# First chunk of a fused attention and gated feed-forward block: scales found from three groups of maxima, weight halves shared between engines, another order around the first gate and up products

## The reference

```python
xn = _layernorm(x)
# attention, 16 heads of 16 channels
q, k, v = split(xn @ Wq.T), split(xn @ Wk.T), split(xn @ Wv.T)
q, k = elu(q) + 1.0, elu(k) + 1.0
kv_state = einsum('bhnd,bhne->bhde', k, v)      # sums over all 1024 tokens
k_state = k.sum(axis=2)
attn = einsum('bhnd,bhde->bhne', q, kv_state) / maximum(einsum('bhnd,bhd->bhn', q, k_state), 1e-6)
local = conv over 3 neighbouring tokens of xn, per channel (conv_w, conv_b)
a = (attn + local) @ Wp.T + bp
# feed-forward, 768 hidden channels, weights int32 in -127..127, scale 1/127
h = silu(xn @ wg.T) * (xn @ wu.T)
out = x + a + h @ wd.T
```

## Time and profile before

| what | us |
|---|---|
| median of 3 runs (507.33 to 507.74) | 507.38 |
| time of the profiled execution | 506.9 |
| its span, first to last instruction | 505.3 |
| TensorE busy (share of the span) | 491.4 (97%) |
| VectorE / ScalarE / GpSimd busy | 430.5 / 334.3 / 144.7 |
| granted TensorE clock, mean | 0.999 |
| mean of one silu, L536 (ScalarE) | 0.687 |
| mean of one hidden, L896 (VectorE) | 0.744 |
| mean of one high half, L544 (ScalarE) | 0.622 |
| mean of one low half, L902 (VectorE) | 0.691 |

### The profile page before, as it was taken

How to read it: one execution, slowest core, us unless ns; L and a number is a source line. 1 busy time by engine, 2 the same in 40 slices (tenths; PEclk the granted TensorE clock), 3 DMA queues, 4 the chain that set the end, 5 groups by cost and what they waited for, 6 DMA issues and landing times.

```text
span 505.3 us, 11017 instructions
## 1 busy us (share of the span) xinstructions
PE 491.4 (97%) x3968; PEld 306.1 (61%) x3968; DVE 430.5 (85%) x833; ACT 334.3 (66%) x522; POOL 144.7 (29%) x152
## 2 busy tenths in 40 slices
PE   7888999999999999999999999999999999999997
PEld 6545364755747566474756657475565756657576
DVE  4889898889888898988889888889888889897786
ACT  2676866667485775757667485667758576674770
POOL 3563415140321405033140502314041141401050
PEclk9999999999999999999999999999999999999999
DMA  8573434333524423252352325233342442233012
GB/s 307 183 91 77 86 82 87 68 111 51 151 43 111 99 45 125 41 166 42 83 125 42 125 42 164 43 82 100 54 138 42 126 82 42 87 50 74 3 42 84
DMA packets 68653, 45.36 MB, mean 90 GB/s; under 512 B 33424, under 2 KB 68112, under 8 KB 68624
## 3 DMA queue, kind: packets, MB, share of 16 engines
q1 hardware_dynamic: 59360, 35.79, 25.2%
q0 software_dynamic: 8448, 8.39, 11.0%
q10 hardware_dynamic: 816, 0.79, 0.5%
HBM read 20.32 MB, written 8.39 MB: 57 GB/s over the span
## 4 chain that ended last, share of the span: by engine, by line
PE 88%; DVE 5%; ACT 3%; DMA 2%; issue 1%; ACTq 0%; DVEq 0%
PE ps L1202 16%; PE ps L1039 16%; PE ps L1211 15%; PE ps L1221 15%; PE ps L1145 15%; PE ps L1101 5%; PE ps L1110 3%; PE ps L1164 2%; DMA wv_raw<-in_L_attn_Wv_dram 2%; DVE maxima L665 1%; DVE hl L902 1%; DVE hid L896 1%; ACT hh L544 1%; DVE cb L764 0%; PE ps L1085 0%
## 5 line engine op out<-in xcount | busy, mean ns | idle before, releaser
L536 ACT ACTIVATE act_g<-ps,scales 128x512 f32<-128x512 f32 x96 | 65.9, 687 | 42.0 <-PE ps L1211 39.7
L896 DVE SCALAR_TENSOR_TENSOR hid<-act_g,scales,ps 128x512 f32<-128x512 f32 x96 | 71.4, 744 | 21.2 <-ACT act_g L536 20.7
L902 DVE TENSOR_TENSOR hl<-hid,hh 128x512 f16<-128x512 f32 x96 | 66.3, 691 | 1.8 <-ACT hh L544 0.4
L361 POOL TENSOR_TENSOR xT<-xh,xl 128x1024 f32<-128x1024 f16 x15 | 32.3, 2153 | 109.4 <-issue 109.4
L544 ACT ACTIVATE hh<-hid 128x512 f16<-128x512 f32 x96 | 59.7, 622 | 5.3 <-DVE hid L896 5.3
L1202 PE MATMUL ps<-xh,g_wh 128*128 128x512 f16 x192 | 57.6, 382 | 2.1 <-ACT u_wh L455 1.4
L1211 PE MATMUL ps<-xl,g_wh 128*128 128x512 f16 x192 | 57.1, 379 | 0.0
L1202 PE MATMUL ps<-xh,u_wh 128*128 128x512 f16 x192 | 57.1, 379 | 0.0
L1211 PE MATMUL ps<-xl,u_wh 128*128 128x512 f16 x192 | 57.1, 379 | 0.0
L1221 PE MATMUL ps<-d_wh,hh 128*128 128x256 f16 x384 | 52.4, 273 | 2.2 <-DVE hid L896 2.2
L499 ACT ACTIVATE k_neg<-ps,scales 128x512 f32<-128x512 f32 x30 | 20.6, 687 | 49.4 <-PE ps L1145 49.4
(11 more groups left out here) (149 smaller groups left out, 965.5 us busy)
## 6 DMA issues: line engine op xcount, KB each, us to landing
xb<-bp_sb SPq DMA_DIRECT2D x16, 512.0 KB, 3.4
xb<-in_L_attn_x_dram POOLq DMA_DIRECT2D x16, 512.0 KB, 5.9
x_in<-in_L_attn_x_dram SPq DMA_DIRECT2D x15, 512.0 KB, 4.1
out_dram<-out_sb SPq DMA_DIRECT2D x14, 512.0 KB, 2.9
out_dram<-out_sb SPq DMA_DIRECT2D x4, 256.0 KB, 2.1
wg_int<-in_L_ffn_w_gate_dram SPq DMA_DIRECT2D x1, 768.0 KB, 7.1
wu_int<-in_L_ffn_w_up_dram SPq DMA_DIRECT2D x1, 768.0 KB, 8.6
wd_int<-in_L_ffn_w_down_dram SPq DMA_DIRECT2D x1, 768.0 KB, 11.1
```

The source lines that it names most:

```text
L536: nc.scalar.activation(act_g[:, j % 2, :], ps[:, gate_bank(j), :], ACT.Silu, scale=silu_in).then_inc(silu_ready, 1)
L896: nc.vector.scalar_tensor_tensor(out=hid[:, j % 2, :], in0=act_g[:, j % 2, :], scalar=h_mul, in1=ps[:, gate_bank(j) + 1, :], op0=ALU.mult, ...
L902: nc.vector.tensor_tensor(hl[:, j, :], hid[:, j % 2, :], hh[:, j, :], ALU.subtract).then_inc(hl_ready, 1)
```

## The change

The down weights' group and the last one become one group, so there are three. VectorE makes the second half of u_wh, ScalarE the first; ScalarE makes v_wh and k_wh, between silu(0) and the first half of the next chunk's x; ScalarE makes four of the six parts of d_wh and GpSimd two. GpSimd adds the first pair of keys once the gate and up weights are ready and the second pair after the next chunk's rstd. On TensorE the turn of the second group has another PSUM bank and waits no more for the first group's scales; its spread stands one place earlier; the two `accumulate` stand behind pairs 2 and 3; the register of the down weights is loaded ahead of `gate_up(5)` instead of ahead of `down(0)`. The scales of the attention need no `powers` of their own. In the second chunk `relu_q` stands ahead of the outer taps. In every chunk GpSimd's sum xT is four instructions. At the end the last output is made and stored in two halves, the second stored from ScalarE's queue.

```diff
-        GROUPS = [["k", "v", "q"], ["g", "u"], ["d"], ["cw", "cb", "p"]]
+        GROUPS = [["k", "v", "q"], ["g", "u"], ["d", "cw", "cb", "p"]]
...
-        MAX_BANK = [7, 7, 7, STATE]
+        MAX_BANK = [7, STATE, 7]
...
             run(sp, step)
+            for c, p in ((0, 0), (0, 1), (1, 0)):
+                store_pair(NB - 1, c, p)
+            sp.wait_ge(out_ready, NB * CB * 2)
+            sp.dma_start(out_v[NB * CB - 1][:, 2, :], out_sb[:, 1, 2, :]).then_inc(out_stored[1], 16)
             for c in range(CB):
-                for p in range(2):
-                    store_pair(NB - 1, c, p)
-            for c in range(CB):
-                sp.wait_ge(out_stored[c], 16 * NB + 16)
+                sp.wait_ge(out_stored[c], 16 * NB + 16 + 16 * c)
...
+                    if c == 1:
+                        first_keys(1)
...
-                nc.gpsimd.tensor_tensor(xT[:, c, :, 1:1 + CHUNK].rearrange("p k (i t) -> p i k t", i=TILES),
-                                        xh[:, c, :, :, :], xl[:, c, :, :, :], ALU.add).then_inc(xT_ready, 1)
+                for i in range(TILES):
+                    ins = nc.gpsimd.tensor_tensor(xT[:, c, :, 1 + i * P:1 + (i + 1) * P], xh[:, c, i, :, :],
+                                                  xl[:, c, i, :, :], ALU.add)
+                ins.then_inc(xT_ready, 1)
...
+            def first_keys(p):
+
                 pool.wait_ge(k_parts, p + 1)
                 nc.gpsimd.tensor_tensor(k_sb[:, 2 * p:2 * p + 2, :], k_exp[:, p, :, :], k_relu[:, p, :, :],
                                         ALU.add).then_inc(k_ready, 1)
+
+            pool.wait_ge(gate_up_seen, 1)
+            pool.sem_inc(norms_due, 1)
+            pool.wait_ge(gate_up_hi, 3)
+            first_keys(0)
...
+                        pool.wait_ge(scaled[2], 1)
+                        pool.sem_inc(norms_due, 1)
+                        nc.gpsimd.tensor_scalar(d_w[0][:, D_BY_ACT:J, :],
+                                                ffn_raw["d"][:, D_BY_ACT * D:J * D].rearrange("p (k n) -> p k n", n=D),
+                                                col(scale_up, "d"), None, ALU.mult).then_inc(d_hi, 1)
...
                 if past:
                     query_parts()
                 else:
-                    high(u_w[0][:, :, :], ffn_raw["u"][:, :].rearrange("p (k n) -> p k n", k=KT), "u", gate_up_hi)
+                    high(u_w[0][:, 0, :], ffn_raw["u"][:, 0:HID], "u", gate_up_hi)
                 nc.scalar.preload_act_table(ACT.Silu)
...
+                    if j == 0 and not past:
+                        high(kv_w[0][:, :, D:2 * D], w_raw["v"][:, :, :], "v", v_hi)
+                        high(kv_w[0][:, :, 0:D], w_raw["k"][:, :, :], "k", k_hi)
                     if j == D_SPLIT and not past:
-                        high(d_w[0][:, :, :], ffn_raw["d"][:, :].rearrange("p (k n) -> p k n", k=J), "d", d_hi)
+                        high(d_w[0][:, 0:D_BY_ACT, :],
+                             ffn_raw["d"][:, 0:D_BY_ACT * D].rearrange("p (k n) -> p k n", n=D), "d", d_hi)
...
             run(act, step)
+            act.wait_ge(out_ready, NB * CB * 2 + 1)
+            act.dma_start(out_v[NB * CB - 1][:, 3, :], out_sb[:, 1, 3, :]).then_inc(out_stored[1], 16)
...
+                nc.vector.tensor_tensor(cb[:, :], cb_raw[:, :], y_up.broadcast_to([P, KT]), ALU.mult).then_inc(taps_made, 1)
+                nc.vector.scalar_tensor_tensor(out=cw[:, :, :], in0=cw_raw[:, :, :], scalar=1.0 / X_UP,
+                                               in1=y_up.unsqueeze(2).broadcast_to([P, KT, 3]), op0=ALU.mult,
+                                               op1=ALU.mult).then_inc(taps_made, 1)
...
+            def last_output(banks):
+
+                dve.wait_ge(wp_done, NB * CB * 2)
+                dve.wait_ge(res_ready, NB * CB * 2)
+                dve.wait_ge(out_stored[1], (NB - 1) * 16)
+                for i in range(2):
+                    nc.vector.scalar_tensor_tensor(out=out_sb[:, 1, 2 + i, :], in0=ps[:, banks[1], i * D:(i + 1) * D],
+                                                   scalar=y_down, in1=res[:, 1, 2 + i, :],
+                                                   op0=ALU.mult, op1=ALU.add).then_inc(out_ready, 1)
...
-                    gate_up_high("g", g_w)
+                    gate_up_high("g", g_w[0][:, :, :], ffn_blocks("g", KT))
+                    gate_up_high("u", u_w[0][:, 1, :], ffn_raw["u"][:, HID:2 * HID])
                     stats(nb, ncx)
-                    weight_maximum("d")
                     gate_up_low_halves()
                     hidden(0)
-                    across(2)
-                    put_state()
+                    weight_maximum("d")
                     hidden(1)
+                    late_maxima()
                     hidden_low(0)
                     hidden(2)
-                    down_scales()
+                    across(2)
                     hidden_low(1)
                     hidden(3)
+                    put_state()
                     hidden_low(2)
-                    late_maxima()
+                    down_scales()
                     hidden(4)
                     hidden_low(3)
                     hidden(5)
                     hidden_low(4)
                     hidden_low(5)
                     down_low_half()
-                    across(3)
...
                 if not attend:
                     put_k(1)
+                    relu_q()
                 tap(pb, pc, 0, 2)
                 tap(pb, pc, 1, 2)
                 if attend:
                     put_k(1)
-                relu_q()
-                if attend:
+                    relu_q()
...
-                if g == len(GROUPS) - 1:
-                    pe.wait_ge(acc_kept, 1)
-                elif g > 0:
-                    pe.wait_ge(scaled[g - 1], 1)
+                if g == 2:
+                    pe.wait_ge(scaled[0], 1)
...
                     turn_maxima(1)
-                    project_first(1, 1)
+                    project_first(1, 1, "k")
                     spread_maxima(1)
+                    project_first(1, 1, "v")
                     project_q()
-                    pe.wait_ge(gate_up_hi, 2)
                     pe.wait_ge(gate_up_seen, 1)
                     is_wide["gate_up"] = pe.value_load(gate_up_wide[0:1, 0:1].bitcast(I32))
+                    pe.wait_ge(gate_up_hi, 3)
                     gate_up(0)
+                    gate_up(1)
+                    gate_up(2)
                     accumulate(0)
+                    gate_up(3)
+                    turn_maxima(2)
                     accumulate(1)
-                    gate_up(1)
-                    turn_maxima(2)
-                    gate_up(2)
                     spread_maxima(2)
-                    gate_up(3)
                     gate_up(4)
-                    gate_up(5)
-                    turn_maxima(3)
-                    pe.wait_ge(hid_ready, J - 1)
-                    pe.wait_ge(d_hi, 1)
                     pe.wait_ge(down_seen, 1)
                     is_wide["down"] = pe.value_load(wide[0:1, 2:3].bitcast(I32))
+                    gate_up(5)
+                    pe.wait_ge(hid_ready, J - 1)
+                    pe.wait_ge(d_hi, 2)
                     down(0, DOWN)
-                    spread_maxima(3)
...
```

76 lines of the change are left out of this document (35 added, 41 removed).

## The result

The changed kernel took 510.56 us (median of 6 executions, 509.43 to 510.91), the kernel before 507.68 in the same comparison: a ratio of 1.0056, 95% interval 1.0046 to 1.0066. It is 0.56% slower; 506.8 was predicted, with a range up to 508.3. The profiled execution took 510.63, its span is 509.0 against 505.3.

A forecast was written before the change was run, and what follows sets the result against it. TensorE, busy almost throughout from 96 to 470 us, was taken as the bound, leaving gains ahead of project_kv's second half (0.44) and at the end (0.10): 0.54 off, so 506.8 us, range 505.0 to 508.3.

The forecast's parts named there:

- Rival 1: VectorE's small statistics not held by GpSimd, xn 0.9 earlier: 505.9, or 505.1 if hidden_low(0) also passes xn_l; chance 0.25.
- Rival 2: Register load ahead of gate_up(5) takes its long 1.41 when DMAs are busy: 507.7; chance 0.14.
- Rival 4: TensorE's waits go as the change's words suggest and no new one comes: 503.7; chance 0.02.
- Rival 3: Second chunk: removing TensorE's wait ahead of gate_up(1) is worth its 0.45: 506.4; chance 0.04.
- down(0) took 2.78 and now takes 2.9 to 3.1: First chunk on TensorE: down(0) lengthens since hidden(5) and its halves come 0.1 to 0.3 late; end 41.74.
- xT in quarters ... Counted: 0: Second chunk and loop: quarters cost GpSimd 0 to 0.6 per chunk, from slack; counted 0, ends 0 to 0.5.
- The rule for the port: VectorE's second port pair is an exclusive lock shared with GpSimd, held per instruction; small statistics' wait taken as 0.87.
- the residual: Ahead of project_kv's second half: x's DMAs, issued about 37.7, land by about 43.5, in time; at longest 46.6, just late.
- at cb: VectorE's scale work after the last hl: ends at 43.5 even with a quarter of GpSimd's sum (0.55) in the way.
- that of 2.3 which the prediction had ahead of gate_up(3): TensorE, done at 27.38, waits 2.3 us for hidden(1); gate_up(3) starts at 29.71, spending the whole 1.49 gained.
- The end: Last output stored in halves: 0.10 gained, with ends of 0.15 lost and 0.4 gained.

The follow-up runs named there:

- the experiment on relu_q: Kernel before with relu_q ahead of the outer taps in the second chunk and the last output in two halves: 506.92 us, ratio 0.9996.

## Why the prediction was wrong, point by point

**Right, up to down(0).**

| place | predicted | after |
|---|---|---|
| gate_up(0) | 21.68 | 22.04 |
| end of the last statistic, held by the key sum | 23.93 | 24.17 |
| gate_up(3) | 29.71 | 29.79 |
| stall of hidden_low(0) beside xn_l | 0.8 | 0.7 |
| gate_up(5) | 36.7 | 36.75 |
| down(0) | 38.67 | 39.00 |

Executions differ by some 0.4 us before any of this: gate_up(0) starts at 22.04 in this profile and at 21.59 in the second one of the same kernel. That gate_up(5) fits is partly luck: the register's value came 0.35 later than forecast (36.33 instead of 35.98), its load was 0.33 shorter (0.32 instead of 0.65). down(0) hangs on the scales and not on that load.

These rows of VectorE show the two stalls that the prediction found, the small statistic (0.17 before) and the low half (0.68):

```profile
22.34 1.01 DVE L633 TENSOR_TENSOR ln_tmp<-bn_raw 128x4 f32<-128x4 f32 x1
...
30.38 1.40 DVE L931 TENSOR_TENSOR hl<-hid,hh 128x512 f16<-128x512 f32 x1
```

Rival 1 falls with the first. Rival 2 did not come: the register load took 323 ns, below both ends of the estimate, 494 and 1408. Its condition was named, though ("when DMAs were busy"), and the 18 profiles bear it out: 317 to 324 ns in the 11 where the transfers that add x come later than the load, 903 to 1446 in the 7 where they run beside it, as before. The change moved them from 30.7 to 38.1 and so made the load short. Rival 4, 503.7, is far off. Rival 3 falls with the experiment on relu_q: from project_kv's second half to the last product it is 454.09 now and was 454.07.

**The step that failed: "down(0) took 2.78 and now takes 2.9 to 3.1"**, and with it "xT in quarters ... Counted: 0". It took 5.46, from the start of down(0) to that of down(1), where the prediction's times have 3.07. The prediction had the DMAs issued at 37.7 instead of 30.7, and asked only whether they land in time for the residual. It did not take the next instruction of the same queue: the sum xT, which before ran from 37.30 and now comes behind the second issue, done at 40.97, beside the last two low halves, which take 3.54 instead of 1.47. I did look for a quarter of the sum beside VectorE, but at cb, one place too late, and priced it as one quarter, 0.55. The rule for the port stood in the prediction; it was applied where the diff moves GpSimd's work (keys, xn_l) and not where the work moves by itself. With that sum out of the way, down(0) takes 3.07 and the time is 507.09, ratio 0.9992, where 506.8 was forecast, a ratio of 0.9989 to the 507.38 shown. The places do not fit as closely: in that profile project_kv's second half starts at 47.76, where 46.97 was forecast, since from gate_up(3) to down(0) it takes 9.89 instead of 9.21, at a granted clock of 0.50 from 30.0 to 33.4. Its three executions with such a mean clock took 506.8 to 507.6, the other eight 506.6 to 507.3, so over many executions no price of a fall at that place shows.

**The second part, not in any step: the clock.** All my estimates took TensorE at full speed, as in every stretch of before. Behind a wait of 2.15 the granted clock fell, and down(1) took 1.65 more. It should have stood as a price beside each new wait, that of 2.3 which the prediction had ahead of gate_up(3) included. The Trainium skill ("TensorE: Matmul & The Clock Gate", section on how the oscillation bites in real kernels) tells of waits between groups of matmuls after which TensorE starts again at its lower clock; the stretches above agree, the second profile of the same kernel, at 1.00 behind the same wait, does not, though it was at 0.50 behind the wait of 1.84 before.

**The balance** of the profiled executions, from before to after, at project_kv's second half: down(0) later 1.87 (39.00 - 37.13); from down(0) to down(1) 5.46 instead of 3.71, 1.75; down(1) longer 1.65 (4.28 - 2.63); project_kv's first half 2.60 instead of 3.94, -1.34. The sum is 3.93, and so is 51.34 - 47.41. Forecast were 1.54, -0.64, 0 and -1.34, so of the 4.37 by which the second half missed its 46.97, 0.33 is down(0)'s start, 2.39 the low halves beside the sum, and 1.65 the clock. The end gives back 0.25 (predicted 0.10): from the last product's start to the end of the span it was 3.82 and is 3.57.

## What to carry to other kernels

When a change puts work into a queue, follow every instruction behind it to its new time, and ask of each what it then runs beside; here the step that moved was not the one that hurt. Price a new wait of TensorE twice, once for itself and once for the clock behind it, and read the mean clock of every execution before calling one profile typical. If one wait takes away a loss, place it: here one wait for the last low half took back 3 us, and with the scales earlier the kernel was 0.35% faster than before.

## What the runs showed of the hardware that was not expected

- A VectorE operation with two inputs in SBUF waited for one instruction of a row on GpSimd (low halves of 0.98 to 1.15 beside quarters of a sum, 1.43 beside a key sum) or through three (3.42 behind GpSimd's DMA issues; 3.66 and 3.67 behind key sums, with no issues). The three came in every profile with the issues right ahead of the quarters, and in two of three beside the late key sums. Issues with no sum behind them held nothing (low halves of 0.68). The cause of the difference is open.
- GpSimd's small sums of two columns show 1.66 and 1.27 behind the issues and 0.20 without them: such a duration is waiting, not work.
- The granted clock fell to 0.50 behind a wait of 2.15 in one profile of the changed kernel and behind one of 1.84 in the other, where it then stayed at 1.00 behind the wait of 2.14. By the mean clock a fall comes in 11 of 12 executions. The place made 0.7 us of difference between the two profiles; the times lie in two groups 1.4 apart.
- TensorE's load of the down register took 317 to 324 ns with no transfer of x beside it and 903 to 1446 ns beside the transfers that add x (512 KB each). Other loads were less regular: VectorE's of the same value took 654 ns beside such a transfer in the kernel before, 1110 in the changed one.
